# Column-counted ring with 1 MB blocks, gathers as one sequence, GpSimd products from step 1, in a recommender tower on one core

## The reference

```python
xk = x0 = e                                   # (b=1024, m=32, d=16)
for W in (W0, W1, W2):                        # (32, 32, 64), (32, 64, 64), (32, 64, 64)
    xk = relu(einsum('bmd,bhd,mhk->bkd', x0, xk, W))
    outs.append(sum(xk, axis=2))              # 64 numbers a sample and layer
h = concatenate([concatenate(outs, axis=1), dense_ctx], axis=1)   # 192 + 16
h = relu(h @ W_top1 + b_top1)                 # 208 -> 512
h = relu(h @ W_top2 + b_top2)                 # 512 -> 256
y = h @ W_top3                                # 256 -> 1
```

## Time and profile before

| | us |
|---|---|
| median of 3 runs | 619.21 (617.38 to 619.29) |
| the profiled execution | 620.28 |
| its span, first to last instruction | 618.5 |
| TensorE matmul busy | 576.0 (93%) |
| VectorE busy | 554.7 (90%) |
| GpSimd busy | 474.4 (77%) |
| ScalarE busy | 306.3 (50%) |

### The profile page before, as it was taken

How to read it: one execution, slowest core, us unless ns; L and a number is a source line. 1 busy time by engine, 2 the same in 40 slices (tenths; PEclk the granted TensorE clock), 3 DMA queues, 4 the chain that set the end, 5 groups by cost and what they waited for, 6 DMA issues and landing times.

```text
span 618.5 us, 8088 instructions
## 1 busy us (share of the span) xinstructions
PE 576.0 (93%) x2716; PEld 205.6 (33%) x2716; DVE 554.7 (90%) x345; ACT 306.3 (50%) x1355; POOL 474.4 (77%) x358
## 2 busy tenths in 40 slices
PE   0899789989999999999999999989999999999997
PEld 0344222323323333333333333333333333333354
DVE  0299899999999999999999999989999999989590
ACT  0133436363547647363555746453565736454442
POOL 6777168979888887889888887988878897949360
PEclk9999999999999999999999999999999999999998
DMA  3777888586776867487876767587775757577000
GB/s 100 238 266 249 324 286 326 207 342 245 310 276 237 289 250 287 154 317 276 314 275 225 304 206 286 195 310 276 285 301 200 306 193 310 218 305 272 1 1 0
DMA packets 35940, 150.89 MB, mean 244 GB/s; under 512 B 7958, under 2 KB 15706, under 8 KB 20538
## 3 DMA queue, kind: packets, MB, share of 16 engines
q1 hardware_dynamic: 27696, 148.26, 63.2%
q0 software_dynamic: 8192, 2.11, 3.0%
q10 hardware_dynamic: 10, 0.00, 0.0%
HBM read 147.20 MB, written 3.15 MB: 243 GB/s over the span
## 4 chain that ended last, share of the span: by engine, by line
DVE 38%; PE 25%; DMA 18%; issue 11%; POOL 4%; SPq 2%; ACT 1%; DVEq 0%; POOLq 0%
DVE prod L364 36%; PE y_ps L546 21%; DMA x0bc<-x_rows 13%; DMA x_rows<-emb 3%; POOL emb L317 3%; DVE z L392 2%; DMA emb<-table,row_sb 2%; POOL pool_prod L332 2%; PE y_ps L560 1%; PE x0g_ps L612 1%; SPq L289 1%; SPq L304 1%; PE x0g_ps L635 0%; SPq L252 0%; PE x0g_ps L617 0%
## 5 line engine op out<-in xcount | busy, mean ns | idle before, releaser
L364 DVE TENSOR_TENSOR prod<-x0bc,x_ps 128x2048 f32<-128x2048 f32 (+2 forms) x272 | 464.1, 1775 | 11.5 <-ACT x_ps L446 11.5
L546 PE MATMUL y_ps<-prod,w_sb 128*64 128x512 f32 (+1 forms) x1792 | 389.6, 566 | 12.3 <-DVE prod L364 11.1
L317 POOL DMA_INDIRECT emb<-table,row_sb x256 | 245.0, 957 | 66.3 <-issue 64.1
L332 POOL TENSOR_TENSOR pool_prod<-x0bc,x_sb 128x1024 f32<-128x1024 f32 x96 | 228.4, 2385 | 58.9 <-ACT x_sb L463 37.1
L546 PEld LDWEIGHTS y_ps<-prod,w_sb 128*64 128x64 f32 x1792 | 123.5, 137 | 254.9 <-issue 203.0
L453 ACT ACTIVATE relu<-y_ps 128x16 f32<-128x16 f32 x480 | 79.6, 292 | 120.7 <-PE y_ps L546 120.7
L446 ACT ACTIVATE x_ps<-y_ps 64x512 f32<-64x512 f32 (+1 forms) x136 | 74.1, 545 | 95.0 <-PE y_ps L546 92.2
L364 DVE TENSOR_TENSOR prod<-x0bc,x0g_ps 128x2048 f32<-128x2048 f32 (+1 forms) x34 | 72.9, 2157 | 29.4 <-DMA x0bc<-x_rows 19.1
L546 PE MATMUL y_ps<-pool_prod,w_sb 128*64 128x512 f32 x384 | 98.6, 594 | 0.7 <-POOL pool_prod L332 0.6
L453 ACT ACTIVATION_READ_ACCUMULATOR relu<-y_ps 128x1 f32 x480 | 79.8, 318 | 0.0
L463 ACT ACTIVATE x_sb<-relu 64x512 f32<-64x512 f32 x120 | 75.4, 629 | 3.2
(11 more groups left out here) (36 smaller groups left out, 80.9 us busy)
## 6 DMA issues: line engine op xcount, KB each, us to landing
x0bc<-x_rows SPq DMA_DIRECT2D x120, 1024.0 KB, 7.3
x0bc<-x_rows SPq DMA_DIRECT2D x16, 512.0 KB, 6.4
x0g<-x_rows SPq DMA_DIRECT2D x15, 512.0 KB
emb<-table,row_sb POOLq DMA_INDIRECT x256
x_rows<-emb SPq DMA_DIRECT2D x15, 128.0 KB
x_rows<-emb SPq DMA_DIRECT2D x17, 64.0 KB
w_sb<-w SPq DMA_DIRECT2D x2, 512.0 KB, 4.3
x0g<-x_rows SPq DMA_DIRECT2D x2, 256.0 KB
```

The costliest lines, as they stand in the source:

```text
L317: pool.indirect_dma_start(emb[:, turn, DIM * n:DIM * (n + 1)], None, table, bass.IndirectOffsetOnAxis(row_sb[:, at:at + 1], 0)).then_inc(g ...
L332: pool.tensor_tensor(pool_prod[:, n % POOL_RING, 0:width(s)], x0bc[:, tile_columns(s, j)], x[:, 0:width(s)], ALU.mult).then_inc(pool_produ ...
L364: made = dve.tensor_tensor(out, left, right, ALU.mult)
L546: made = pe.matmul(ps[MAPS * h:MAPS * (h + 1), 0:half(s)], w, moving[:, half(s) * h:half(s) * (h + 1)], start=first, stop=final)
```

## The change

- **Ring.** It is counted in columns (24 times 1024), and every transfer is one block of 2048 columns, 1 MB. In steps 0 and 1 that is four tiles rather than two, and those steps take 8192 columns each rather than 16384. Which earlier tiles a block has to wait for is computed by `last_in_place`, and how many arrivals a semaphore must show by `landed`.
- **Gathers.** They are one sequence over all steps, taken in order. 32 (steps 0 to 2) run ahead of the first product, not 48. `MORE_GATHERS` gives the numbers in steps 1 and 2; later steps keep 1, 1, 8 and 1, 1, 4. By the end of step 2 they stand at 66, before at 64.
- **Products.** GpSimd makes the last 3 tiles of both layers in step 1, and in step 2 the last 2 of layer 1 (3 before) and the last 3 of layer 2.
- **Perceptron weights** are loaded after steps 2, 3 and 4, not 1, 2 and 3.
- **Start.** 3 unused matmuls ahead of layer 0 of step 0 and 2 behind it, before 7 and 3.

The diff, without the lines that only rename:

```diff
-MOVED = 2
+BLOCK = 2 * PAIR
 X0_ROWS = FIELDS + max(SHIFT)


-SLOTS = 24
+RING_COLUMNS = 24 * PAIR
 RING = 4
 POOL_RING = 4

-POOL_OF = {0: (0, 0), 1: (0, 0), STEPS - 2: (5, 4), STEPS - 1: (5, 4)}
+POOL_OF = {0: (0, 0), 2: (2, 3), STEPS - 2: (5, 4), STEPS - 1: (5, 4)}
 POOL_COUNT = [POOL_OF.get(s, (3, 3)) for s in range(STEPS)]
-POOL_BEFORE = {0: [], 3: [2, 3, 5], 4: [2, 3, 4, 5], 5: [2, 3, 4, 5, 5]}
+POOL_BEFORE = {0: [], 2: [3, 5], 3: [2, 3, 5], 4: [2, 3, 4, 5], 5: [2, 3, 4, 5, 5]}
+
+
+GATHERED_FIRST = 32
 GATHERS_AFTER = {1: [1, 1, 8], 2: [1, 1, 4]}
-
-GATHERED_FIRST = 4
+MORE_GATHERS = {(1, 1): [0, 0, 6], (1, 2): [0, 0, 10], (2, 1): [0, 11], (2, 2): [1, 1, 5]}
...
+def first_column(s, j):
+
+    return TILES * DIM * FIRST_ROW[s] + width(s) * j
+
+
 def tile_columns(s, j, count=1):

-    lead = j - j % MOVED
-    at = PAIR * ((TILES * s + lead) % SLOTS) + width(s) * (j - lead)
+    at = first_column(s, j) % RING_COLUMNS
     return slice(at, at + width(s) * count)
+
+
+def moved(s):
+
+    return BLOCK // width(s)
+
+
+def landed(s, j):
+
+    return 16 * sum(1 for i in range(s % 2, s + 1, 2) if TILES // moved(i) > j // moved(s))
+
+
+def last_in_place(s, j):
+
+    a = first_column(s, j) - RING_COLUMNS
+    found = [(i, t) for i in range(s + 1) for t in range(TILES)
+             if a < first_column(i, t) + width(i) and first_column(i, t) < a + BLOCK]
+    by_pool = [x for x in found if x[1] in pool_tiles(x[0], 2)]
+    by_vector = [x for x in found if x not in by_pool]
+    return by_vector[-1:], by_pool[-1:]
...
             def wait_free(s, j):

-                own = range(j, j + MOVED)
-                by_pool = [t for t in own if t in pool_tiles(s, 2)]
-                by_vector = [t for t in own if t not in by_pool]
-                if by_pool:
-                    sp.wait_ge(pool_products, pool_before((s, 2)) + pool_tiles(s, 2).index(by_pool[-1]) + 1)
-                if by_vector:
-                    sp.wait_ge(products, before((s, 2)) + by_vector[-1] // GROUP + 1)
+                by_vector, by_pool = last_in_place(s, j)
+                for i, t in by_vector:
+                    sp.wait_ge(products, before((i, 2)) + t // GROUP + 1)
+                for i, t in by_pool:
+                    sp.wait_ge(pool_products, pool_before((i, 2)) + pool_tiles(i, 2).index(t) + 1)

             def load_tiles(s):
                 store_at, load_at = AHEAD.get(s, (TILES, TILES))
-                for j in range(0, TILES + MOVED, MOVED):
+                for j in range(0, TILES + 1, moved(s)):
                     if s + 1 < STEPS:
                         if j == store_at:
                             store_rows(s + 1)
@@ -281,12 +306,11 @@
                             load_x0g(s + 1)
                     if j == TILES:
                         break
-                    k = TILES * s + j
-                    if k >= SLOTS:
-                        wait_free(*divmod(k - SLOTS, TILES))
+                    wait_free(s, j)
                     rows = bass.AP(x0_rows.tensor, rows_at(s) + SHIFT[j] * width(s),
-                                   [[width(s), FIELDS], [0, QUART], [1, MOVED * width(s)]])
-                    sp.dma_start(x0bc[:, tile_columns(s, j, MOVED)], rows).then_inc(bc_in[s % 2][j // MOVED], 16)
+                                   [[width(s), FIELDS], [0, QUART], [1, BLOCK]])
+                    sp.dma_start(x0bc[:, tile_columns(s, j, moved(s))], rows
+                                 ).then_inc(bc_in[s % 2][j // moved(s)], 16)
...
-                for dst, src in {1: ((wt1a_sb[:], wt1_a),),
-                                 2: ((wt1b_sb[:], wt1_b), (wt3_sb[:], wt3), (bt1_sb[:], bt1), (bt2_sb[:], bt2)),
-                                 3: ((wt2_sb[:], wt2), (zt_b[MAPS:, :], dense_t))}.get(s, ()):
+                for dst, src in {2: ((wt1a_sb[:], wt1_a),),
+                                 3: ((wt1b_sb[:], wt1_b), (wt3_sb[:], wt3), (bt1_sb[:], bt1), (bt2_sb[:], bt2)),
+                                 4: ((wt2_sb[:], wt2), (zt_b[MAPS:, :], dense_t))}.get(s, ()):
...
-            def gather(s, a, b):
-                turn = s % 2
-                if a == 0 and s >= 2:
-
-                    pool.wait_ge(scratch_out[turn], 32 * (s // 2))
-                for n in range(a, b):
-                    at = FIRST_ROW[s] // QUART + n
+            all_gathers = iter([(s, n) for s in range(STEPS) for n in range(GATHERS_OF[s])])
+
+            def gather(count):
+                for s, n in islice(all_gathers, count):
+                    turn, at = s % 2, FIRST_ROW[s] // QUART + n
+                    if n == 0 and s >= 2:
+
+                        pool.wait_ge(scratch_out[turn], 32 * (s // 2))
                     pool.indirect_dma_start(emb[:, turn, DIM * n:DIM * (n + 1)], None, table,
                                             bass.IndirectOffsetOnAxis(row_sb[:, at:at + 1], 0)
                                             ).then_inc(gathered[turn], 16)
@@ -321,29 +346,26 @@
             def layer(s, l, x):
                 if not pool_tiles(s, l):
                     return
-                gathers = GATHERS_AFTER[l]
-                done = 0 if l == 1 else sum(GATHERS_AFTER[1])
+                gathers = MORE_GATHERS.get((s, l), GATHERS_AFTER[l])
                 pool.wait_ge(copied[l - 1], copies_after(s, l - 1))
                 for k, j in enumerate(pool_tiles(s, l)):
-                    pool.wait_ge(bc_in[s % 2][j // MOVED], 16 * (s // 2 + 1))
+                    pool.wait_ge(bc_in[s % 2][j // moved(s)], landed(s, j))
                     n = pool_before((s, l)) + k
                     if n >= POOL_RING:
                         pool.wait_ge(pool_products_used, n - POOL_RING + 1)
                     pool.tensor_tensor(pool_prod[:, n % POOL_RING, 0:width(s)], x0bc[:, tile_columns(s, j)],
                                        x[:, 0:width(s)], ALU.mult).then_inc(pool_products, 1)
-                    if GATHERED_FIRST <= s + 2 < STEPS:
-                        gather(s + 2, done, done + gathers[k])
-                        done += gathers[k]
+                    if k < len(gathers):
+                        gather(gathers[k])

             pool.wait_ge(ids_in, 32)
             for cols in (slice(0, GATHERS_OF[0]), slice(GATHERS_OF[0], BATCH // QUART)):
                 pool.tensor_tensor(row_sb[:, cols], ids_sb[:, cols],
                                    off_sb[:].to_broadcast([P, cols.stop - cols.start]), ALU.add).then_inc(rows_done, 1)
             pool.wait_ge(rows_done, 1)
-            gather(0, 0, GATHERS_OF[0])
+            gather(GATHERS_OF[0])
             pool.wait_ge(rows_done, 2)
-            for s in range(1, GATHERED_FIRST):
-                gather(s, 0, GATHERS_OF[s])
+            gather(GATHERED_FIRST - GATHERS_OF[0])
...
-            keep_going((0, 0), 7)
+            keep_going((0, 0), 3)
             layer0(0)
-            keep_going((0, 1), 3)
+            keep_going((0, 1), 2)
```

9 lines of the change are left out of this document (5 added, 4 removed).

## The result

| | before | changed |
|---|---|---|
| median of 6 runs | 619.16 us (617.38 to 619.94) | 615.64 us (613.53 to 615.96) |
| profiled execution | 620.28 us | 615.86 us |
| its span | 618.5 us | 614.0 us |
| mean granted clock | 0.996 | 0.989 |

The ratio of the times is 0.9941, with a 95% interval from 0.992 to 0.9963. The kernel is faster by 3.5 us in the medians and by 4.4 us between the two profiled executions. The forecast was 7.1 us. The difference is 0.6%, and the interval leaves out 1. In the trace after, lines 317, 332, 364, 546 and 560 have become 342, 356, 386, 568 and 582.

What follows compares the result with a forecast made beforehand. VectorE sets the pace but for 9.2 us of waiting for tiles, TensorE close behind. 0.4 + 2.2 + 4.3 + 0.2 = 7.1 us: 613.2 profiled, 612.1 beside the median; forecast's own range 610.3 to 614, overall 608.5 to 617.5.

Steps and rivals of the forecast that it cites:

- The stalls in the even part: VectorE's waits ahead of layer 0, 9.2 us from 120 to 560 us; gathers two ahead should remove all later ones.
- the 1.5 us to spare: Even part: with gathers 2.5 us earlier the loop takes 32.9 us against VectorE's 34.43, leaving this slack.
- Step 3's gathers: Gathers behind step 1's products: layer 0 of step 3 at 92.4, VectorE idle from 87.5, 0.4 us of gain left.
- The rival in which step 3's gathers are sooner: Shorter path to x2 or faster half products: up to 4.9 us more gain, 607.2 to 611 us; chance 0.08.
- the one in which they collide with step 2's tiles: Step 2's transfers still under way at step 3's gathers and store: 12.1 us slower, 624.2 us; chance 0.06.
- TensorE in the even part: Steps 8 to 14: of VectorE's 5.1 us of waits, 4.3 gained, as TensorE has only 4.2 us idle.
- 0.2 for step 16: Gain at layer 0 of step 16: VectorE's stall is 1.81 us, but TensorE has 0.45 us idle in all.
- 0.4 + 2.2 = 2.6: Gain by step 6: 0.4 us left by step 3, 2.2 us from stalls ahead of layer 0 of steps 4 and 6.
- The rival that TensorE holds the even part: Even part: the 4.3 us gain becomes 2, since TensorE has the same matmuls to do; 614.4 us, chance 0.12.
- The start and TensorE's clock: Shorter run of unused matmuls, some 2.5 us idle: nothing taken; rival of a slow start costs 2 us, 614.1, chance 0.13.
- The 1 MB block: Layer 0 of step 0 waits for one block landing at about 26.2; TensorE ends about 0.4 us later, bounds 0 and 1.2.
- The row from which I argued: Layer 0 of step 2: 8 matmuls took 1.94 us after 3.17 us idle, taken as a sign that idling does not matter.

Runs made afterwards that it cites:

- Taking the lead back: Changed kernel with two gathers fewer behind layer 2 of step 2 (3 rather than 5), so they stand at 64 again; 617.98 us, ratio 1.0001.

## Where the prediction was right, and where not

*The stalls in the even part.* Right in the main. The loop of gathers, store, x0g and tiles was 0.97 us too long, 2.5 us were taken out of it, and of 9.2 us of stalls 7.3 went. Layer 0 of steps 4 and 5, and of 5 and 6, lie 34.35 us apart ((196.70 - 128.00) / 2), the forecast being 34.4. Taking the lead back brought stalls and time back. At step 16 VectorE had won 6.6 us, beside 7.1 in the whole sum.

Not all of the 1.5 us to spare was there. Ahead of step 12 VectorE still idled for 0.80 + 0.21 us, where I had put none. That turn of the loop took 35.2 us from layer 0 of step 11 (369.26) to that of step 12 (404.49). The gathers came 2.5 us sooner, as meant. But x2 was there after 8.99 us and not 8.18, the store began 3.2 us behind the last gather for step 12 (389.16) and not 2.5, and from x0g to the first product it took 9.74 us and not 8.94:

```profile
394.75 0.52 SPq L289 DMA_DIRECT2D x0g<-x_rows  x1
```

So where TensorE is behind and the transfers land late, the 2.5 us are used up again.

*Step 3's gathers.* The mechanism was right, step by step: the copy of x2 was to be there at 64.8, the last gather to go at 79.7, the store at 82.2, x0g at 84.6 and the first tiles at 92.4. GpSimd and SyncE show:

```profile
64.28 3.76 POOL L356 TENSOR_TENSOR pool_prod<-x0bc,x_sb 128x512 f32<-128x512 f32 x3 [5.54 <-ACT x_sb L485]
...
79.45 0.94 POOL L342 DMA_INDIRECT emb<-table,row_sb  x1 [0.30 <-issue]
```

```profile
81.73 0.86 SPq L279 DMA_DIRECT2D x_rows<-emb  x2
84.07 0.52 SPq L289 DMA_DIRECT2D x0g<-x_rows  x1
```

All of it came about 0.5 us early or less. The term that was mis-sized is the last: from x0g to the first product it took 93.00 - 84.07 = 8.93 us and not 7.85. I had taken the row of step 3 before over that of step 6 (8.94). So 0.2 us were lost by step 3, where 0.4 were to be won. The rival in which step 3's gathers are sooner, and the one in which they collide with step 2's tiles, did not come about. That VectorE would idle 5 us there stood in the forecast as a price to be paid. The runs show that it was the largest gain left: closing it took 3.3 us more.

*TensorE in the even part.* I counted 4.3 us for steps 8 to 14, because TensorE had 4.2 us of idle time to give, and 0.2 for step 16. On VectorE it was more; TensorE gave less. Its first perceptron matmuls in step 6 and in the last step, before:

```profile
205.42 0.70 PE L606 MATMUL x0g_ps<-zt_a,wt1a_sb 128*128 128x256 f32 x2
...
587.59 0.59 PE L606 MATMUL x0g_ps<-zt_a,wt1a_sb 128*128 128x192 f32 x2
```

After:

```profile
203.37 0.70 PE L628 MATMUL x0g_ps<-zt_a,wt1a_sb 128*128 128x256 f32 x2
...
582.31 0.59 PE L628 MATMUL x0g_ps<-zt_a,wt1a_sb 128*128 128x192 f32 x2
```

It had won 2.05 us by the first (forecast: 0.4 + 2.2 = 2.6) and 5.28 by the second, 3.2 between them where I had 4.5. The windows between these two points, before and after:

```profile
205.42:587.59 382.17, 377.44 (x1718) 130.94 (x1716) 367.62 (x214) 206.29 (x953) 312.84 (x221) 1.00 0.68 254
```

```profile
203.37:582.31 378.94, 375.68 (x1719) 131.21 (x1717) 367.28 (x214) 207.48 (x955) 311.43 (x220) 1.00 0.69 256
```

TensorE's idle time fell only from 4.7 to 3.3 us; the other 1.8 of the 3.2 us are less busy time for the same matmuls. I had let it give all of its idle time. Part of what is left goes with the stall ahead of step 12 (0.57 us idle from 400 to 440 us), part with the gap on GpSimd at 462.98, behind which TensorE waits for GpSimd's products (0.90 us from 440 to 480). Neither was in the forecast. The term that was mis-sized is that of the even part: I read that TensorE sets the end, put 0.2 us on step 16 for it, and did not ask how far VectorE may run ahead before TensorE's queue is what counts. The rival that TensorE holds the even part is refuted in its place (412.65 us with and without a part of its load) and has the right sign for the tail.

*The start and TensorE's clock.* The 1 MB block was to land at 26.2 and cost 0.4 us; VectorE started at 25.24, and layer 1 of step 0 at 30.51 where it was 30.13 before. So 0.4 us came, but by luck. With the longer run of unused matmuls the same block let layer 0 of step 0 end at 29.00, sooner than the 29.24 of before: the block cost nothing, and the 0.4 us are TensorE's clock, for which I had taken nothing. The window of 20 to 40 us shows a mean granted clock of 0.91, where it was 1.00 before:

```profile
20.00:40.00 20.00, 15.62 (x86) 6.18 (x86) 11.84 (x12) 4.11 (x9) 15.12 (x17) 0.91 0.89 336
```

Here 16 matmuls took 3.11 us where 15 of the same took 2.05 with the longer run. The Trainium skill, "TensorE: Matmul & The Clock Gate", section "HAM oscillation — how this bites in real kernels", has the burst behind an idle gap begin at the lower clock. This trace agrees that the clock falls there, but not that the burst begins slow: the granted clock was 1.00 until 27.5 us, one microsecond into the burst, and 0.50 (1.2 GHz) from there to 31 us. In the kernel with four gathers ahead it fell at 26.2 us, ahead of the burst, and the 16 took 3.68 us. The clock of the changed kernel fell again at step 3, where it was 0.50 from 95.8 to 99.2 us:

```profile
95.35 5.35 PE L568 MATMUL y_ps<-prod,w0s_sb 128*64 128x512 f32 x16 [2.85 <-DVE prod L386]
```

In the repeated changed kernel these 16 ran at full speed (1.94 us for each 8), and layer 0 ended 7.1 us behind VectorE's start of it, here 7.7: it cost 0.6 us. The row from which I argued, 3.17 us of idle time with no loss behind it, was true and did not carry; behind 2.85 us the clock fell. That the first unused matmuls ran at the lower level rests on their length alone, since the granted clock is 1.00 from 18 us on.

*The end.* The last chunk's 16 matmuls took 2.78 us in the profiled execution of before and 3.61 in that of after.

```profile
612.99 2.78 PE L635 MATMUL x0g_ps<-h,wt_sb 128*128 128x64 f32 x16 [0.40 <-ACT h L487]
```

```profile
607.71 3.61 PE L657 MATMUL x0g_ps<-h,wt_sb 128*128 128x64 f32 x16 [0.40 <-ACT h L509]
```

The repeat of the changed kernel, without any edit:

```profile
608.82 2.64 PE L657 MATMUL x0g_ps<-h,wt_sb 128*128 128x64 f32 x16 [0.41 <-ACT h L509]
```

In the kernel with four gathers ahead they took 2.00, in that without products in step 1 2.35, with the same code there. So this 0.8 us is where the clock happened to fall in these two executions, and not an effect of the change: before the change it fell at 614 us, with about half of these matmuls to go, after it at 608, with nearly all.

**The sum as it came.** Forecast 7.1 us. By step 6, 0.55 less (mostly the tiles of step 3); from there to the last step 1.3 less on TensorE; at the last chunk 0.8 less, by chance. That makes 4.45, and the spans are 4.5 apart. In the medians it is 3.5, since the profiled execution of before lay 1.1 us above its median and that of after 0.2. I had taken 1.1 off both. So the sign, the mechanism and the place of the new stall were right, and the size was twice what came. The 615.64 us lie outside the 610.3 to 614 that I gave to the forecast itself. They lie within 608.5 to 617.5 only because that range was drawn wide for the rivals, none of which came about as put.

## What to carry to other kernels

Where one engine paces the even part and another is 98% busy beside it, write down for each how long its own work takes from the last common point to the end: what the first wins beyond the second's slack is given back in the tail. And where a forecast finds a new idle time of 5 us as the price of a change, that is a part to take out of the change: here moving four instructions was worth as much as the whole of it.
